# Layer 1 in one block, and the weighted sums of attention two units at a time

## The reference, cut to what matters

```python
def _L1_attn_ref(x, Wq, Wk, Wv, Wo):       # b=2, t=1024, H=32 heads of 16, HKV=8, G=4
    q, k, v = heads(x @ Wq.T), heads(x @ Wk.T), heads(x @ Wv.T)
    q = q * cos + _rotate_half(q) * sin
    k = k * cos + _rotate_half(k) * sin
    scores = einsum('bhgtd,bhkd->bhgtk', qg, k) / sqrt(DH)      # causal
    attn = softmax(where(causal, scores, -max))
    ctx = einsum('bhgtk,bhkd->bhgtd', attn, v)
    return out @ Wo.T

def _L1_ffn_ref(x, ...):                   # weights of 4 bits, INTER=1376
    w_gu = sc[g_idx] * (wq - zq[g_idx])    # the same for w_d
    gate, up = split(x @ w_gu)
    return (silu(gate) * up) @ w_d
```

## Time and profile before

| | |
|---|---|
| median of 3 runs | 1502.73 us (1500.64 to 1506.34) |
| the profiled execution | 1504.61 us, its span 1502.9 us |
| layer 0 | until about 345 us of the span |
| projections of layer 1 | about 360 to 472 us |
| feed-forward part | 477 to about 915 us |
| attention, 16 groups | about 925 to 1446 us |
| output | 1446 to 1503 us |
| mean granted clock of TensorE | 0.943 of full speed |

### The profile page before, as it was taken

The page is one execution under the profiler, slowest core; times in us unless marked ns, Lnnn a source line. Parts: engine busy times, 40 slices in busy tenths (PEclk is TensorE's granted clock), DMA queues, the critical chain, the costliest instruction groups (busy, mean ns, idle before and its releaser), DMA issues.

```text
span 1502.9 us, 20829 instructions
## 1 busy us (share of the span) xinstructions
PE 1353.9 (90%) x6642; PEld 929.9 (62%) x6642; DVE 1067.0 (71%) x2495; ACT 618.9 (41%) x859; POOL 334.0 (22%) x387
## 2 busy tenths in 40 slices
PE   3788988982995599999999997999999999999998
PEld 2556776762773477777777774555555555555467
DVE  6887977774774555555554477888888888888547
ACT  4643755442441011111111111566666666666652
POOL 2753566541321000000000000222212222212211
PEclk9878998985998699999999995999999999999999
DMA  6111200005343100000000050111112132221002
GB/s 218 51 46 39 85 0 29 0 29 188 110 123 115 43 21 22 21 22 22 22 21 17 5 95 0 33 33 33 33 34 59 39 89 60 61 62 32 2 29 84
DMA packets 45315, 76.22 MB, mean 51 GB/s; under 512 B 9572, under 2 KB 16948, under 8 KB 45220
## 3 DMA queue, kind: packets, MB, share of 16 engines
q1 hardware_dynamic: 43086, 73.36, 17.7%
q10 hardware_dynamic: 2134, 1.69, 0.4%
HBM read 55.73 MB, written 19.01 MB: 50 GB/s over the span
## 4 chain that ended last, share of the span: by engine, by line
PE 58%; DVE 5%; issue 1%; ACT 1%; DVEq 1%; DMA 0%; SPq 0%; POOL 0%; ACTq 0%; POOLq 0%
PE d_bank L1817 11%; PE d_bank L1857 9%; PE d_bank L37 9%; PE d_bank L1841 9%; PE d_bank L39 8%; PE d_bank L38 8%; DVE d_bank L1633 2%; PE d_bank L1865 1%; DVE mx_first L1636 1%; DVEq L1639 1%; PE d_bank L1743 1%; DVE hl L1591 0%; DVE hs L1588 0%; ACT hh L1490 0%; PE d_bank L1885 0%
## 5 line engine op out<-in xcount | busy, mean ns | idle before, releaser
L1526 ACT ACTIVATE prob<-d_bank 128x1024 f32<-128x1024 f32 (+3 forms) x384 | 303.2, 811 | 222.0 <-PE d_bank L1841 217.7
L1633 DVE CUSTOM_DVE_ANT_0 d_bank<-d_bank,mask 128x128 f32<-128x128 f32 (+3 forms) x512 | 247.3, 503 | 61.3 <-PE d_bank L1817 55.3
L1817 PE MATMUL d_bank<-kst,qst 96*128 96x512 f32 (+3 forms) x768 | 268.4, 390 | 5.9 <-DVE mx_first L1636 2.8
L1817 PEld LDWEIGHTS d_bank<-kst,qst 96*128 96x128 f32 x768 | 145.5, 193 | 153.6 <-DVE mx L1633 56.4
L1841 PE MATMUL d_bank<-qst,kst 98*128 98x512 f32 (+3 forms) x768 | 211.9, 359 | 0.2 <-ACT prob L1526 0.2
L1452 POOL TENSOR_SCALAR_AFFINE_SELECT prob<-prob 128x256 f32<-128x256 f32 x256 | 104.1, 407 | 460.3 <-ACT prob L1526 458.5
L1636 DVE TENSOR_REDUCE mx_first<-d_bank 128x1 f32<-128x512 f32 x256 | 176.3, 688 | 17.4 <-PE d_bank L1817 12.6
L1857 PE MATMUL d_bank<-prob,vst 128*32 128x512 f32 (+3 forms) x1536 | 165.6, 503 | 1.2 <-POOL prob L1452 1.2
L1482 ACT ACTIVATE hs<-d_bank 128x512 f32<-128x512 f32 (+1 forms) x44 | 26.3, 598 | 339.2 <-PE d_bank L39 339.2
L37 PE MATMUL d_bank<-xtl,wgh 128*128 (+1 forms) x352 | 141.3, 402 | 8.8 <-DMA zz<-z_gu_scr 8.8
L1841 PEld LDWEIGHTS d_bank<-qst,kst 98*128 98x128 f32 x768 | 130.4, 192 | 19.3 <-ACT prob L1526 9.6
(11 more groups left out here) (256 smaller groups left out, 2435.3 us busy)
## 6 DMA issues: line engine op xcount, KB each, us to landing
wst<-L_ffn_w SPq DMA_DIRECT2D x8, 1024.0 KB, 6.6
qst<-q_scr SPq DMA_DIRECT2D x32, 256.0 KB, 4.7
qw<-L_ffn_qweight_gu SPq DMA_DIRECT2D x40, 128.0 KB, 2.6
xb<-L_attn_x SPq DMA_DIRECT2D x4, 1024.0 KB, 6.7
x_d<-xb SPq DMA_DIRECT2D x4, 1024.0 KB, 4.3
c_xb<-x_d SPq DMA_DIRECT2D x4, 1024.0 KB, 7.5
q_scr<-c_qh SPq DMA_DIRECT2D x16, 256.0 KB
q_scr<-c_ql SPq DMA_DIRECT2D x16, 256.0 KB
```

The costliest lines, as they stand in the source:

```text
L1526: act.activation(prob[:, c // 2 % 2, c % 2 * 2:c % 2 * 2 + 2, lo:], score_bank[c % 2][:, :, lo:], ACT.Exp, scale=D ** -0.5).then_inc(exp_d ...
L1633: dve.tensor_tensor_reduce(sc, sc, mask[:, CH - w:CH], 1.0, LEAST, ALU.add, ALU.max, mx[:, u, h % 2, h // 2, q:q + 1]).then_inc(spare_free, 1)
L1817: pe.matmul(spare_bank(number)[:, 0:w], qst[u][0:M_ROW, h // 2, q * P:q * P + P], kst[u][0:M_ROW, h % 2, at:at + w], start=True, stop=True ...
```

## The change

It does three things.

1. `layer1_projections` and `layer1_rest` become one block, `layer1`, without the barrier. Tiles are placed by hand, so that those of the projections and of the feed-forward part can live side by side. The six pieces of step 0 are made inside the projections: TensorE's row matmuls at the places of `ROWS`, VectorE's work at those of `MADE`, SP's loads at those of `LOADS`, into banks 6 and 7 for the scales and zeros. The comparison that makes `hot_gu` and `hot_d` moves from the end of chunk 2 to chunk 1.
2. To make room, the normalized tokens overwrite the loaded ones, tokens are turned through two banks and no longer three, the sine product stays in its bank, and the sum of a rope goes where the cosine product was. `ident` is loaded once.
3. In attention `weighed` is called for two units one after the other in every fourth step, and `prob` keeps four units.

```diff
+        MADE = {(1, 2): 0, (2, 0): 1, (2, 2): 2, (3, 0): 3, (3, 2): 4, (3, 4): 5}
+        ROWS = {(1, 2): 0, (2, 1): 1, (2, 3): 2, (3, 1): 3, (3, 3): 4, (3, 5): 5}
+        LOADS = {(1, 3): (2,), (2, 3): (3, 4), (3, 1): (5,)}
...
+        probs = [place(f"prob{i}", [P, 2, HG, CH], F32, at) for i, at in enumerate((147.5, 187.5))]
...
+        def prob(i):
+            return probs[i // 2 % 2][:, i % 2]
...
-                    pool.wait_ge(rope_ready, r + 1)
+                    if r >= 2:
+                        pool.wait_ge(ql_ready, r - 1)
...
-                    dve.tensor_tensor(qs[:, r % 2], bank[:, 4 + r % 2], sin[:, u * CH:u * CH + CH], ALU.mult)
+                    dve.tensor_tensor(bank[:, 4 + r % 2], bank[:, 4 + r % 2], sin[:, u * CH:u * CH + CH], ALU.mult)
...
-                    dve.tensor_tensor(qs[:, r % 2], qs[:, r % 2], qc[:, r % 2], ALU.add).then_inc(rope_ready, 1)
+                    dve.tensor_tensor(qc[:, r % 2], bank[:, 4 + r % 2], qc[:, r % 2], ALU.add).then_inc(rope_ready, 1)
...
+                    if (c, m) == (1, 0):
+                        hot_groups()
+                        dve.drain()
+                        pick(0, 0)
+                    if (c, m) in MADE:
+                        n = MADE[c, m]
+                        if n == 0:
+                            dve.wait_ge(s_out, 96)
+                        piece(0, n // 3, *PIECES[n % 3])
+                        if n == 2:
+                            pick(0, 1)
...
+            turn_values(CHUNKS - 1)
+            pe.wait_ge(qf_ready, CHUNKS * OT + 2)
+            pe.wait_ge(rope_ready, CHUNKS * ROT + 2)
+            pe.wait_ge(v_ready, CHUNKS + 1)
             each_pair(pe, body)
...
-                    if c % 2 == 0 and n * NU + c // 2 >= 2:
-                        act.wait_ge(av_done, n * NU + c // 2 - 1)
+                    if c % 2 == 0 and n * NU + c // 2 >= 4:
+                        act.wait_ge(av_done, n * NU + c // 2 - 3)
...
-                    if c > 1 and c % 2 == 1:
-                        weighed(n, c // 2 - 1)
-                    elif c == 1 and n > 0:
-                        weighed(n - 1, NU - 1)
+                    if c % 4 == 1:
+                        for i in (c // 2 - 2, c // 2 - 1):
+                            if i >= 0 or n > 0:
+                                weighed(n if i >= 0 else n - 1, i % NU)
...
+            weighed(NG - 1, NU - 2)
             weighed(NG - 1, NU - 1)
```

More of the change, by code:

```diff
@@ new lines, with beside @@
+HEAD = 3
+ITEMS = [(h, q, at, min(CH, (q + 1) * P - at)) for h in range(HG) for q in range(QB) for at in range(0, (q + 1) * P, CH)]
+NI = len(ITEMS)
+TURN_MAXIMA = 19
+TURN_FIRST_HALF = 10
+LOADED = 8 * 16
+LEAST = -3.0e38
+SPARE = 3
+BESIDE = 32
+def beside(c):
+    cost = [w + 96 for *_, w in ITEMS]
+    upto = lambda x: sum(sum(cost[:s + 1]) <= sum(cost) * x / NC + 1e-6 for s in range(len(ITEMS)))
+    at = (c - TURN_MAXIMA) % NC
+    return range(upto(at), upto(at + 1))
+EARLY = beside(NC - 1).stop
@@ new lines, in tasks @@
+def tasks(ahead):
+    out = []
+    for c in range(NC):
+        if c < TURN_MAXIMA and ahead >= 1:
+            out += [(c, "items", s) for s in beside(c)]
+        if c == HEAD - 1:
+            out.append((c, "turn the group before", None))
+        if c == TURN_FIRST_HALF:
+            out.append((c, "turn half", None))
+        if c >= TURN_MAXIMA and ahead >= 2:
+            out += [(c, "early", s) for s in beside(c)]
+        if c == TURN_MAXIMA and ahead >= 1:
+            out.append((c, "turn maxima", None))
+    return out
@@ new lines, in freed, with todo, span @@
+        def freed(number):
+            return number - 1 if number < NI else number if number < NI + SPARE else number - SPARE + 1
+        def todo(n, c):
+            for at, (cc, task, s) in enumerate(tasks(ahead_of(n))):
+                if cc == c and not (n == 0 and task == "turn the group before"):
+                    yield use(n, at + (1 if n == 0 and c < HEAD else 0)), task, s
+        def prob(i):
+            return probs[i // 2 % 2][:, i % 2]
+        def span(h, k):
+            return max(0, k * P - h * CH)
@@ L992, in _, with round_rope @@
             high_parts(0, range(TPC))
-            def high_part(c, k):
+            def round_rope(c, k):
                 r = rope(c, k)
@@ L1197 @@
-EARLY = beside(NC - 1).stop
-def tasks(ahead):
-    out = []
-    for c in range(NC):
-        if c < TURN_MAXIMA and ahead >= 1:
-            out += [(c, "items", s) for s in beside(c)]
-        if c == HEAD - 1:
-            out.append((c, "turn the group before", None))
-        if c == TURN_FIRST_HALF:
-            out.append((c, "turn half", None))
-        if c >= TURN_MAXIMA and ahead >= 2:
-            out += [(c, "early", s) for s in beside(c)]
-        if c == TURN_MAXIMA and ahead >= 1:
-            out.append((c, "turn maxima", None))
-    return out
```

924 lines of the change are left out of this document (441 added, 483 removed).

## The result

The changed kernel takes 1529.21 us (median of 4 runs, 1524.51 to 1532.52), the kernel before 1502.88 in the runs beside it: a ratio of 1.0178, 95% interval 1.0147 to 1.0209. It is slower by 26 us, clear of the noise; the prediction said slower by 18, 1521 us, within 1474 to 1536. The profiled execution took 1532.52 us, its span 1530.8.

The account below looks back on a forecast made before the run. TensorE seemed to set the pace in attention, with VectorE close behind at 26.4 of 32.1 us a group. Attention +39 and seam -21 gave +18 on the median of 1502.7: 1521 us, range 1474 to 1536.

Parts of the forecast that it names:

- the step that I had worked out instant by instant: Attention, burst of step 13 to the next: eight items through three banks take 4.77 us instead of 4.25.
- Attention: Paired visits make a group 34.9 us instead of 32.1, 39 us later in all; bounds 29 earlier to 48 later.
- the stretches with a normalization: Two of a group's six stretches between bursts, said to lose most, 0.8 and 0.7 us, from VectorE's ten or more items' work.
- The saved switch: Attention: going into the 32-column tiles and back costs TensorE 0.31 us a visit; six fewer visits free 1.86 us a group.
- Rival A: Attention: TensorE is the bound throughout and visits cost a mode switch; attention -29, seam -21, 1453 us; chance 0.12.
- the seam's: Layer 1, projections to feed-forward: one block brings the first gate matmul 21 us earlier, at 486.8; bounds 16 to 26.
- The cheaper add: Ropes in the projections: an add reading one operand from a bank takes 0.69 us, not 0.97, saving 4.2 us.
- The pieces' size: Projections: each piece of dequantized weights costs VectorE 3.6 us; five and the picking add 18.6 us.
- The idle time: Projections: of VectorE's 21.5 us idle, 8.9 us of waits for TensorE and GpSimd can be filled with pieces.
- Behind the last rope: Seam: 5 us until SP sees the last stores and sixth piece done, then 3.2 us for the scales.
- C: Seam: pieces don't fit among the ropes, VectorE holds TensorE; seam worth 8 us at most, 1534 us; chance 0.08.
- my own case: Whole kernel: 1505 us (seam -26, attention +28) to 1535 us (seam -16, attention +48); chance 0.58.

Follow-up runs that it names:

- single visits, same steps: The changed kernel with attention's weighted sums called for one unit at a time again, four units' exponentials still kept: 1491.53 us, ratio 0.9938 to the kernel before.
- unread items, pairs: The changed kernel, paired visits, with VectorE writing a zero column instead of reading each item for row maxima from group 1 on: 1446.47 us, ratio 0.9612.
- pieces behind, late scales: One block, single visits, all six pieces of step 0 made behind the last rope instead of five among the ropes: 1497.54 us, ratio 0.9967.
- pieces behind, early scales: One block with all six pieces behind the last rope, plus step 1's scales sent for once the first piece is done: 1494.09 us, ratio 0.9949.
- pieces among, early scales: One block, single visits, pieces as in the changed kernel, step 1's scales sent for in chunk 2 instead of behind the last store: 1490.09 us, ratio 0.9912.
- the two shifted kernels: One block, single visits, early scales, pieces moved behind the next chunk's low parts: first three at ends of chunks 0 to 2, 1488.51 us; none in chunk 0, 1491.23.
- two narrow pairs a group: One block, early scales, single visits except units 2 and 3 together and units 7 and 8 together: 1485.85 us, ratio 0.9892.

## Why the prediction was right, and where it was not

**The sign and most of the size** come from the step that I had worked out instant by instant: eight items through three banks between two bursts. Stretches of a group, from the end of a burst to the end of the next, medians of 6 to 12 groups:

| to the burst in step | 5 | 9 | 13 | 17 | 21 | 1 | sum |
|---|---|---|---|---|---|---|---|
| predicted | 6.51 | 4.61 | 6.84 | 4.77 | 6.37 | 5.84 | 34.9 |
| the changed kernel | 6.53 | 4.69 | 6.64 | 4.85 | 6.20 | 5.62 | 34.5 |
| single visits, same steps | 5.68 | 4.39 | 6.13 | 4.26 | 5.98 | 5.67 | 32.1 |
| unread items, pairs | 5.15 | 3.89 | 5.70 | 3.84 | 5.10 | 5.59 | 29.3 |

No stretch is off by more than 0.22 us. Attention was put at 39 us later; the pairs cost 37.1 in two blocks and 37.7 in one. As said, VectorE starved 6.7 us a group. Of the stretches with a normalization, said to lose most, the one to step 5 lost 0.85, but the one to step 13 only 0.51, less than the 0.59 of the stretch to step 17. That VectorE's reading is the cause is shown, not argued: with items unread the same pairs gain 24 us. That three banks are the limit was not varied.

**The saved switch** was put at 0.31 us; 0.28 is what it measures when nothing else binds. Rival A was thus right about what a visit costs and wrong that TensorE is the bound. The Trainium skill, "TensorEngine Tiling (Array Packing)", Key Properties, says that a change of tiling mode drains TensorE; the 0.28 agrees. Even without the items A's 29 us aren't reached: a group gets 1.23 us shorter, not 1.86.

**The step that failed is the seam's**: "18.6 - 8.9 - 4.2 = 5.5 us later, if all idle time can be filled", the last rope at 478.6 and the gate matmul 21 us earlier. In us from the second statistics, with TensorE's granted clock in the first chunk from there, in the second, and from there to the last rope:

| | clock | last rope | gate matmul |
|---|---|---|---|
| before, two profiles | 0.94, 1.00, 1.00 | 97.0, 97.1 | 133.9, 133.9 |
| pieces among the ropes, late scales, two profiles | 1.00, 1.00, 0.97 | 110.2, 110.2 | 119.8, 119.8 |
| the same, two more | 0.94, 0.94, 0.96 | 113.3, 113.4 | 123.1, 123.1 |
| the same, the changed kernel and one more | 0.89, 0.89, 0.96 | 116.4, 116.3 | 126.1, 125.9 |
| pieces behind, late scales | 1.00, 1.00, 1.00 | 95.7 | 123.3 |
| pieces behind, early scales | 0.94, 1.00, 1.00 | 97.2 | 123.0 |
| pieces among, early scales, two profiles | 1.00, 1.00, 0.97 and 0.94, 0.94, 0.96 | 110.2, 113.4 | 115.6, 118.7 |

- The cheaper add. It is cheaper: L1561 took 0.69 us each (692 ns) where L1104 took 967. But at the same clocks the last rope came at 97.2 with no pieces among the ropes and at 97.0 before the change: of the 4.2 us nothing is to be seen. TensorE, busy 70.2 of 74 us before, kept its pace. What the add alone was worth can't be told from the other changes in that block, such as the turns through two banks. The Trainium skill's page "SBUF — State Buffer", section Who interferes with whom, has it that a VectorE instruction with two SBUF inputs contends with a GpSimd one that reads SBUF; the 967 and 692 ns agree.
- The pieces' size. The 3.6 us were the distance of pieces that waited for TensorE's row matmuls; one among the ropes, or the first behind them, takes 3.2, so the new work was 16.4 us instead of 18.6 with a picking of 0.4.
- The idle time. At full clock in the first two chunks, five pieces and the picking moved the last rope from 95.7 to 110.2, by 14.5 us (at 0.97 instead of 1.00 behind them): about 2 of 16.4 were hidden, not 8.9. TensorE waits for VectorE's low parts and VectorE for TensorE's rotation; what delays one takes the other's slack too. That TensorE stands still at the chunks' starts is seen (6.4 us in two waits, against 1.6 with the pieces behind). That the place of the pieces, and not their sum, makes the loss is not shown: the two shifted kernels gained nothing, with waits of their own that make them a poor test.
- Behind the last rope I had 8.2 us from its end; from the start of its last subtraction it is 9.6 to 9.8, 8.9 to 9.1 from its end, as the last store takes 5.07 to land before SP looks at the scales. Early scales take 4.3 of it away.

The seam's 21 us were thus 8 to 14 in the profiles and 11.4 in the medians, below the 16 to 26 that I allowed. How much of it needs pieces among the ropes is open. By the profiles hardly any: with them behind, the gate matmul still comes 10.6 us sooner, without the barrier and with SP's first loads ahead. By the medians half: 1497.54 against 1491.53, and 1494.09 against 1490.09 with early scales. C put the seam at 8 at most, because VectorE would hold TensorE; it does hold it, and the size lies between C's and mine.

With attention at 37 instead of 39 and the seam at 11 instead of 21, +18 became +26. That the time still fell into the range is in part luck: the range went up to 48 for attention, which it didn't need, and that made room for the seam. The lower end of my own case, 28 for attention, was given without a working.

## What to carry to other kernels

Before joining two bursts of one engine, ask how much work its partner has queued at the burst's start and how many buffers hold it: while a burst lasts longer than that queue the partner starves, and when both engines are near the bound that comes back as waits of the first. Work it out instant by instant with measured durations, it is worth the page; the rule alone did not foretell what two narrow pairs a group would gain. "Idle time can be filled" needs the same care: in a loop in which two engines wait for each other, count only what the loop doesn't hand on, here about a quarter of it. Take the length of a piece of work without its waits. And look at what the queue that issues a late DMA stands behind: moving two DMAs ahead of the last stores brought the gate matmul 4 us closer to the last rope, though the times don't yet show it clear of the noise.

## What the runs showed of the hardware

The same projections differ by up to 6 us between executions of the same code (110.2 to 116.4, from six profiles in three pairs), and TensorE's granted clock differs with them, as the table above has it. Windows of 6 us after layer 0, of the changed kernel:

```profile
364.00:370.00 6.00, 3.35 (x15) 2.82 (x16) 2.67 (x4) 3.22 (x7) 0.00 (x0) 0.50 0.75 234
370.00:376.00 6.00, 3.59 (x20) 2.99 (x19) 4.44 (x7) 3.31 (x6) 0.00 (x0) 0.78 0.04 14
376.00:382.00 6.00, 6.00 (x15) 4.66 (x15) 5.66 (x22) 0.88 (x2) 2.72 (x5) 0.52 0.45 163
```

and of the one block with single visits:

```profile
364.00:370.00 6.00, 4.37 (x26) 3.61 (x24) 4.05 (x6) 3.22 (x6) 0.00 (x0) 0.73 0.10 37
370.00:376.00 6.00, 4.54 (x22) 3.64 (x20) 5.52 (x16) 1.45 (x3) 1.25 (x2) 1.00 0.58 178
376.00:382.00 6.00, 6.00 (x26) 4.24 (x25) 4.88 (x16) 2.69 (x5) 3.79 (x5) 1.00 0.02 1
```

From 376 to 382 both are busy throughout; at a granted clock of 0.52, near the lower level of 1.2 GHz, TensorE gets 15 instructions done, at 1.00 (2.4 GHz) 26. In the 12 us ahead of that it had been busy for 6.9 in the first and 8.9 in the second. The chunk (from the second statistics to the third) takes 28.7 us in the one and 25.8 in the other, and in the next the clock is 0.89 against 1.00 and the chunk 32.1 against 29.0. So a seam of a few us can't be read from a single profile unless the clocks are alike: my first reading, 6 us, lay 5 below the 11 of the medians.
